# Two expert stages on chunks of 1024 tokens instead of 512, GRU weights loaded before the attention, head sums added block by block

## The chip, the core and the metric

The kernel runs on one core of a Trainium2 chip. The metric is the device time in microseconds. The kernel before took 2214.73 us (median of three runs, 2214.09 to 2214.98). The core has five engines, each with its own instruction queue: TensorE (PE, matmuls into PSUM), VectorE (DVE), ScalarE (ACT), GpSimd (POOL) and SyncE (SP), which here only issues DMAs. They wait for one another through semaphores.

## What is computed

The input is x, 4096 tokens of 128 features, and a 4096 x 4096 adjacency matrix. Four blocks follow one another, each on the layer-normed x, each added to x:

```python
x = x + gnn0(layernorm(x), adj)   # 3 attention heads over adj, two GRU cells
x = x + ffn0(layernorm(x))        # 1 shared and 8 routed experts, width 512, gelu, top 2
x = x + gnn1(layernorm(x), adj)   # adj @ bilinear(h), relu
x = x + ffn1(layernorm(x))        # 8 routed experts, width 256, relu, top 2

# ffn0 (ffn1 has no shared expert, and relu)
h = gelu(einsum('sd,edf->sef', x, W1) + b1)
y = einsum('sef,efd->sed', h, W2) + b2
out = shared + einsum('sed,se->sd', y, mask)   # mask: weights of the two chosen experts

# gnn0
edge_output = gru(adj @ h, h); node_output = gru(sum_of_heads / 3, h)
```

All experts are computed for all tokens; the mask is zero for those not chosen.

## The kernel before

Features lie on the 128 partitions and tokens along the free axis, so x is a tile `xT` of 128 x 4096. The order of the work on every engine is written out by hand, and semaphores tie the engines together; nothing is planned by a scheduler.

**Attention.** `adj` is read in four column blocks of 1024 (`RB`), each in 32 row tiles. For each tile SyncE loads `Ab` (the piece of adj) and `Tt` (weights); GpSimd takes out the diagonal where the tile has one, and in any case raises `a_prep`; ScalarE makes `ss` and rounds `Ab` to bf16 (`Ahi`), after `a_prep`; VectorE makes the remainder `Alo` and the products `ph` and `pl`; TensorE does 24 matmuls. `ph` and `pl` have two buffers each. After a block VectorE and ScalarE evacuate PSUM (`esP`, one part for each head, and `nsT`). After the last block GpSimd adds the three head parts, 512 columns at a time (lines 458 and 460), and SyncE loads the GRU weights and the diagonal `dB`; VectorE and TensorE begin the GRU when `g_in` counts all three.

**GRU.** Sixteen units of 512 columns; TensorE makes four PSUM banks of a unit with fp32 matmuls, ScalarE and VectorE the gates, GpSimd multiplies by `dB` and adds to `xT`.

**Expert stages** (`ffn_tensor`, `ffn_scalar`, `ffn_vector`, `ffn_loads`; k is 0 or 1). First the router: TensorE makes the logits, VectorE picks the two largest, ScalarE makes one `exp` (line 675), TensorE transposes the mask (line 948), ScalarE copies it (`mk8`), and SyncE writes it to DRAM and loads it back broadcast to all partitions (`mB`). Around the router the loop begins early: one expert (k = 0) or two (k = 1) are sent up before the transposes. ScalarE works on four units of them before it comes to `exp`.

The main loop runs over eight chunks of 512 tokens, and in each over nE experts with nF pieces of 128 hidden features (9 and 4, then 8 and 2). For each piece ("unit") TensorE's `up` does three matmuls of 512 columns (bf16 high and low parts) into one PSUM bank out of four; ScalarE's `hidden` applies bias and gelu or relu into `hid` (four buffers) and makes the bf16 copy `hidp` (line 659, every second one in stage 0, where VectorE makes the other, line 1373; all in stage 1); VectorE makes the remainder (line 1382). `down` does three matmuls per unit into the expert's PSUM bank. VectorE's `weighted` adds the bias and multiplies by the mask row (`yT`, line 1401) and adds to `xT` (line 1404). TensorE sends expert e + 1 (stage 0) or e + 2 (stage 1) up before expert e goes down. The mask rows lie in two halves of eight buffers (one chunk each); a chunk's first `weighted` waits for all eight of its half.

The lines below fix how far TensorE may run ahead; `act_done` starts at `HB` = 4.

```python
act.sem_inc(act_done[k], HB)
pe.wait_ge(act_done[k], q * (nE * nF) + j + 1)       # up: a free PSUM slot
act.wait_ge(hid_lo[k], q * (nE * nF) + j + 1)        # hidden: a free hid buffer
pe.wait_ge(hid_lo[k], q * (nE * nF) + HB + (e + 1) * nF)   # down: all units of the expert split
```

Of the kernel before, what the change touches and what calls it, by code (L numbers as in the profile page):

```python
# [9 lines left out]
ALU = mybir.AluOpType  # L10
# [3 lines left out]
ds = bass.ds  # L14
# [9 lines left out]
HB = 4  # L24
TS = 4
# [31 lines left out]
def build(nc, a, out):  # L57
    with ExitStack() as ctx:
# [110 lines left out]
        gruW = sb("gruW", [P, 4, 3 * P], F32, 32)  # L169
        gruB = sb("gruB", [P, 4, 3], F32, 39)  # L170
        gbr = sb("gbr", [P, 2, 2], F32, 39.5)
# [5 lines left out]
        Wr = sb("Wr", [P, NE], F32, 56)  # L177
        rb2 = sb("rb2", [P, 2, NE], F32, 56.25)
# [86 lines left out]
        mB_in = [S("mB_in00", "mB_in01"), S("mB_in10", "mB_in11")]  # L265
# [14 lines left out]
        def _(sp):  # L280
# [85 lines left out]
            sp.dma_start(gruW[:, :, :], a["gruW"]).then_inc(g_in, 16)  # L366
            sp.dma_start(gruB[:, :, :], a["gruB"]).then_inc(g_in, 16)
            sp.dma_start(dB[:, :], diag_d.partition_broadcast(P)).then_inc(g_in, 16)

            def ffn_loads(k, nE, nF):  # L370
# [11 lines left out]
                sp.dma_start(mk_d[k][:, 0:2 * CH], mk8[:, 0:2 * CH]).then_inc(r_out, 16)  # L382
                sp.wait_ge(r_out, 32 * k + 16)
                def weights(s, q):
                    for e in range(NE):
                        sp.dma_start(mB[:, NE * s + e, :], mk_d[k][e, ds(q * CH, CH)].partition_broadcast(P)
                                     ).then_inc(mB_in[k][s], 16)

                weights(0, 0)
                sp.wait_ge(r_mk8, 4 * k + 4)  # L390
                sp.dma_start(mk_d[k][:, 2 * CH:], mk8[:, 2 * CH:]).then_inc(r_out, 16)
                sp.wait_ge(r_out, 32 * k + 32)
                sp.wait_ge(mB_in[k][0], 16 * NE)
                weights(1, 1)
# [7 lines left out]
            sp.wait_ge(dve_ffn0, NC * (2 * NE + 1))  # L402
# [14 lines left out]
            sp.wait_ge(dve_ffn1, NC * 2 * NE)  # L417
# [6 lines left out]
        def _(pool):  # L424
# [12 lines left out]

            for rb in range(NRB):
# [96 lines left out]
        def _(act):  # L535
# [111 lines left out]
            def ffn_scalar(k, nE, nF, func):  # L647
# [4 lines left out]

                act.sem_inc(act_done[k], HB)
                ring = (12, 8)[k]

                def high(q, j):
                    act.wait_ge(act_done[k], q * (nE * nF) + HB + j + 1)
                    act.wait_ge(down_done[k], q * nE + j // nF + 1)
# [27 lines left out]
                for j in range(HB, nE * nF):  # L686
                    hidden(NC - 1, j)
# [865 lines left out]
```

## Time and profile before

The profiled execution took 2213.51 us; its span from the first to the last instruction is 2211.7 us. The stages by their place in it:

| stretch, us | what | TensorE busy | VectorE busy | granted clock |
|---|---|---|---|---|
| 380 to 1080 | attention | 665.5 | 608.8 | 0.98 |
| 1080 to 1094 | last evacuation, loads for the GRU | 0.8 | 4.1 | 0.64 |
| 1094 to 1190 | GRU | 90.3 | 59.9 | 0.96 |
| 1214 to 1246 | router, first expert stage | 24.5 | 16.8 | 0.68 |
| 1246 to 1618 | loop of the first expert stage | 366.6 | 325.5 | 1.00 |
| 1779 to 1955 | adj @ bilinear | 174.4 | 142.1 | 0.99 |
| 1990 to 2030 | router, second expert stage | 25.0 | 18.0 | 0.76 |
| 2030 to 2204 | loop of the second expert stage | 159.0 | 158.3 | 1.00 |

From the page:

```profile
PE 1821.4 (82%) x8950; PEld 875.2 (40%) x9101; DVE 1692.5 (77%) x1792; ACT 1398.9 (63%) x1767; POOL 187.9 (8%) x154
PE   4221573799999999999798899999987789997997
DVE  4555427788898888888467688888859988855898
PEclk7555788899999999999897899999989999988999
```

The first line is busy time and share of the span of each engine with its number of instructions (PEld is TensorE's weight load, which lies beside its matmuls). The others cut the span into 40 equal slices: a digit is the busy share in tenths, in the last line the granted TensorE clock, where 10 tenths are 2.4 GHz and 5 are 1.2 GHz. An engine's idle time costs nothing unless another waits for it.

### The profile page before, as it was taken

How to read it: one execution, taken by the hardware profiler on the slowest of the kernel's cores; microseconds unless marked ns; L12 is line 12 of the kernel's file. 1: busy time of each engine (PE TensorE's matmuls, PEld its weight loads, DVE VectorE, ACT ScalarE, POOL GpSimd, SP SyncE). 2: the span in 40 equal slices, each digit the busy share in tenths (PEclk: the TensorE clock that was granted, in tenths of full speed). 3: DMA queues.
4: the chain of work that ended last, by engine and by line, in shares of the span. 5: the costliest groups of instructions: out<-in, count | busy, mean ns of one | idle time of the engine just before them, and what ended most of it. 6: DMA issues, size and time to landing. Idle time of an engine off the chain costs nothing.

```text
span 2211.7 us, 30420 instructions
## 1 busy us (share of the span) xinstructions
PE 1821.4 (82%) x8950; PEld 875.2 (40%) x9101; DVE 1692.5 (77%) x1792; ACT 1398.9 (63%) x1767; POOL 187.9 (8%) x154
## 2 busy tenths in 40 slices
PE   4221573799999999999798899999987789997997
PEld 4111221344444444444345444444452234463332
DVE  4555427788898888888467688888859988855898
ACT  1777006778787787788334566776645567626885
POOL 0000001100000000000442000000017710000000
PEclk7555788899999999999897899999989999988999
DMA  5997025454545544554600311232030079814532
GB/s 166 429 427 319 0 80 205 162 155 150 170 150 156 169 148 154 170 151 149 238 0 0 79 38 39 48 60 45 1 123 11 0 305 429 366 39 81 98 89 76
DMA packets 79575, 313.89 MB, mean 142 GB/s; under 512 B 13958, under 2 KB 14438, under 8 KB 69494
## 3 DMA queue, kind: packets, MB, share of 16 engines
q1 hardware_dynamic: 79500, 312.98, 42.5%
q8 instruction: 36, 0.59, 0.1%
q14 instruction: 39, 0.32, 0.1%
HBM read 297.88 MB, written 15.08 MB: 142 GB/s over the span
## 4 chain that ended last, share of the span: by engine, by line
PE 40%; DVE 9%; POOL 3%; issue 3%; ACT 1%; DMA 1%; DVEq 0%; SPq 0%; POOLq 0%; ACTq 0%
PE psum L926 9%; PE psum L936 8%; PE psum L1008 7%; PE psum L876 7%; POOL halves L487 3%; DVE hidp L1382 2%; DVE xT L1404 2%; DVE yT L1401 2%; DVE prod L1441 2%; PE psum L900 1%; PE psum L902 1%; PE psum L748 1%; PE psum L914 1%; PE psum L743 1%; PE psum L754 1%
## 5 line engine op out<-in xcount | busy, mean ns | idle before, releaser
L589 ACT ACTIVATE ss<-KR,dpt 128x1024 bf16<-128x1024 int16 x384 | 413.1, 1138 | 112.0 <-DVE pl L1274 111.2
L876 PE MATMUL psum<-ph,Tt 128*128 128x512 bf16 x1502 | 411.9, 380 | 8.8 <-DVE pl L1274 7.0
L665 ACT ACTIVATE hid<-psum,fB 128x512 f32<-128x512 f32 x416 | 271.2, 686 | 151.2 <-PE psum L926 108.0
L936 PE MATMUL psum<-hidp,fW 128*128 128x512 bf16 x1215 | 289.2, 381 | 23.3 <-DVE hidp L1382 17.3
L926 PE MATMUL psum<-hTp,fW 128*128 (+1 forms) x1224 | 295.3, 384 | 5.9 <-ACT mk L679 2.8
L1382 DVE TENSOR_TENSOR hidp<-hid,hidp 128x512 bf16<-128x512 f32 x416 | 268.7, 687 | 26.7 <-DVE xT L1404 10.4
L1271 DVE TENSOR_TENSOR ph<-ss,Ahi 128x3072 bf16<-128x3072 bf16 x128 | 225.2, 1760 | 61.9 <-PE psum L876 60.2
L876 PE MATMUL psum<-pl,Tt 128*128 128x512 bf16 x752 | 225.9, 380 | 0.8
L876 PEld LDWEIGHTS psum<-ph,Tt 128*128 128x128 bf16 x1536 | 150.5, 98 | 190.4 <-issue 6.4
L1274 DVE TENSOR_TENSOR pl<-ss,Alo 128x3072 bf16<-128x3072 bf16 x128 | 224.2, 1751 | 0.0
L936 PEld LDWEIGHTS psum<-hidp,fW 128*128 128x128 bf16 x1248 | 117.6, 98 | 183.2 <-issue 42.1
L926 PEld LDWEIGHTS psum<-hTp,fW 128*128 128x128 bf16 x1248 | 123.2, 99 | 155.1 <-issue 12.1
L1268 DVE TENSOR_TENSOR Alo<-Ab,Ahi 128x1024 bf16<-128x1024 f32 x128 | 163.2, 1275 | 17.3 <-ACT Ahi L599 17.3
L876 PE MATMUL psum<-Ahi,Tt 128*128 128x512 bf16 x503 | 151.0, 380 | 24.2 <-DVE Alo L1268 20.3
L659 ACT ACTIVATE hidp<-hid 128x512 bf16<-128x512 f32 x272 | 163.4, 624 | 0.0
L1468 DVE TENSOR_TENSOR A4lo<-A,A4hi 128x4096 bf16<-128x4096 f32 x32 | 141.3, 4425 | 21.5 <-ACT A4hi L719 21.5
L541 ACT ACTIVATE Ar<-Ar 128x4096 f32<-128x4096 f32 x32 | 115.7, 3617 | 58.2 <-DVE keep L1102 58.2
L719 ACT ACTIVATE A4hi<-A 128x4096 bf16<-128x4096 f32 x32 | 115.4, 3616 | 50.0 <-PE psum L1008 23.2
L599 ACT ACTIVATE Ahi<-Ab 128x1024 bf16<-128x1024 f32 x128 | 133.3, 1042 | 6.4 <-issue 6.3
L785 PE MATMUL psum<-uvs,keep 128*128 128x18 bf16 x1024 | 32.7, 176 | 122.0 <-DVE keep L1102 122.0
L1008 PE MATMUL psum<-A4hi,Xb 128*128 128x512 bf16 x512 | 115.9, 379 | 0.0
L986 PE MATMUL psum<-bw,h3b 128*128 128x512 bf16 x368 | 86.1, 385 | 34.2 <-DVE prod L1441 32.5
(228 smaller groups left out, 2110.6 us busy)
## 6 DMA issues: line engine op xcount, KB each, us to landing
Ar<-in_adjT SPq DMA_DIRECT2D x32, 2048.0 KB, 12.9
Ab<-in_adjT SPq DMA_DIRECT2D x128, 512.0 KB, 4.1
A<-in_adjT SPq DMA_DIRECT2D x32, 2048.0 KB, 11.1
Tt<-T_d SPq DMA_DIRECT2D x128, 256.0 KB, 2.6
mB<-mk_d SPq DMA_DIRECT2D x128, 256.0 KB, 7.6
T_d<-tb SPq DMA_DIRECT2D x32, 256.0 KB, 2.0
RD<-rden_d SPq DMA_DIRECT2D x12, 512.0 KB, 5.3
fWs<-in_W SPq DMA_DIRECT2D x2, 2304.0 KB, 16.5
```

Source lines behind the costliest of these rows:

```text
L589: last = nc.scalar.activation(ss[s % 2][:, h, :], KR[:, h, rb * RB:(rb + 1) * RB], ACT.Sigmoid, scale=STEP, bias=dpt[:, ds(t * HEADS + h, 1)])
L659: nc.scalar.activation(hidp[j % ring][:, 0, :], hid[j % HB][:, :], ACT.Copy).then_inc(hid_hi[k], 1)
L665: nc.scalar.activation(hid[j % HB][:, :], psum[:, j % HB, :], func, bias=fB1[:, j:j + 1]).then_inc(act_done[k], 1)
L876: last = nc.tensor.matmul(psum[:, 2 * h + q, :], Tt[s % AS][:, h, w, :], mv[:, q * CH:(q + 1) * CH], start=fresh and k == 0, stop=False, s ...
L926: last = nc.tensor.matmul(psum[:, j % HB, :], fW[0][x][:, j * P:(j + 1) * P], hTp[y][:, nlast(q)], start=(w == 0), stop=(w == 2))
L936: last = nc.tensor.matmul(psum[:, HB + e % dn, :], fW[1][x][:, j * P:(j + 1) * P], hidp[j % ring][:, y, :], start=(f == 0 and w == 0), sto ...
L1008: last = nc.tensor.matmul(psum[:, q, :], Xb[w][:, ds(n, 1), :].rearrange("p o f -> p (o f)"), mv[s][:, q * CH:(q + 1) * CH], start=False, ...
L1268: V.tensor_tensor(Alo[s % AS][:, :], Ab[s % AS][:, :], Ahi[s % AS][:, :], ALU.subtract).then_inc(a_lo, 1)
L1271: V.tensor_tensor(ph[s % 2][:, :, :], ss[s % 2][:, :, :], Ahi[s % AS][:, :].unsqueeze(1).to_broadcast([P, HEADS, RB]), ALU.mult).then_inc( ...
L1274: V.tensor_tensor(pl[s % 2][:, :, :], ss[s % 2][:, :, :], Alo[s % AS][:, :].unsqueeze(1).to_broadcast([P, HEADS, RB]), ALU.mult).then_inc( ...
L1382: V.tensor_tensor(hidp[j % ring][:, 1, :], hid[j % HB][:, :], hidp[j % ring][:, 0, :], ALU.subtract).then_inc(hid_lo[k], 1)
L1468: V.tensor_tensor(A4lo[s][:, :], A4[s][:, :], A4hi[s][:, :], ALU.subtract).then_inc(l_lo, 1)
```

## The change

1. **Expert stages.** A chunk is 1024 tokens (`CW`), so the loop has four rounds (`NW`). A unit takes two PSUM banks: the `up` slots are banks 0-1 and 2-3, two instead of four, and an expert's output banks 4-5 or 6-7, two instead of three or four. Each weight is used by two matmuls in a row (`for b in range(2)`). ScalarE's, VectorE's instructions and the mask DMAs are 1024 columns wide and half as many. `hid` stays four buffers, each twice as wide, and `hidp` has nine. `down` waits unit by unit.
2. **Mask rows.** Eight buffers `mB`, each refilled for the next chunk when its expert is done; `weighted` waits for pairs of them.
3. **GRU weights** are loaded to another place, ahead of `rden_d` and so of the attention; `dB` is counted by `x_in`, for which only GpSimd waits. TensorE no longer waits for the third head's evacuation.
4. **Head sums**: `head_sums(rb - 1)` behind the tiles of block rb, the last one at the end.

```diff
-            pe.wait_ge(es_out, HEADS * NRB + 1)
+            pe.wait_ge(es_out, HEADS * NRB)
...
-            sp.dma_start(dB[:, :], diag_d.partition_broadcast(P)).then_inc(g_in, 16)
+            sp.dma_start(dB[:, :], diag_d.partition_broadcast(P)).then_inc(x_in, 16)
...
+            def head_sums(rb):
+                pool.wait_ge(es_out, HEADS * rb + HEADS + 1)
+                for q in range(rb * RB // CH, (rb + 1) * RB // CH):
+                    c = slice(q * CH, (q + 1) * CH)
+                    pool.tensor_tensor(esT[:, c], esT[:, c], esP[:, 1, c], ALU.add).then_inc(es_add, 1)
+                    pool.wait_ge(es_add, q + 1)
+                    pool.tensor_tensor(esT[:, c], esT[:, c], esP[:, 2, c], ALU.add).then_inc(es_ok, 1)
...
+                if rb > 0:
+                    head_sums(rb - 1)
+
+            head_sums(NRB - 1)
+            pool.wait_ge(x_in, 48)
...
-                with sp.Fori(1, NC // 2) as i:
-                    for s in range(2):
-
-                        sp.wait_ge(y_used[k], (2 * i + s - 1) * nE + (3, 4)[k])
-                        weights(s, 2 * i + s)
+                with sp.Fori(1, NW) as q:
+                    for e in range(NE):
+                        sp.wait_ge(y_used[k], (q - 1) * nE + (nE - NE) + e + 1 + 2)
+                        weights(q, e)
...
-                act.sem_inc(act_done[k], HB)
-                ring = (12, 8)[k]
+                act.sem_inc(act_done[k], 2)
+                ring, hold = (9, 8)[k], (3, 4)[k]
...
-                    nc.scalar.activation(hid[j % HB][:, :], psum[:, j % HB, :], func,
+                    nc.scalar.activation(hid[j % HB][:, :], flat[:, j % 2 * CW:j % 2 * CW + CW], func,
...
-                            last = nc.tensor.matmul(psum[:, j % HB, :], fW[0][x][:, j * P:(j + 1) * P],
-                                                    hTp[y][:, nlast(q)], start=(w == 0), stop=(w == 2))
+                            for b in range(2):
+                                last = nc.tensor.matmul(psum[:, j % 2 * 2 + b, :], fW[0][x][:, j * P:(j + 1) * P],
+                                                        hTp[y][:, ds(q * CW + b * CH, CH)], start=(w == 0),
+                                                        stop=(w == 2))
...
-                    pe.wait_ge(hid_lo[k], q * (nE * nF) + HB + (e + 1) * nF)
-                    pe.wait_ge(y_used[k], q * nE + e + 1)
+                    pe.wait_ge(y_used[k], q * nE + e + (2 if nE % 2 and e == 0 else 1))
                     for f in range(nF):
                         j = e * nF + f
+                        pe.wait_ge(hid_lo[k], q * (nE * nF) + HB + j + 1)
...
-                    if e == nE - NE:
-                        dve.wait_ge(mB_in[k][half], (i + 1) * (16 * NE))
+                    if p >= 0 and p % 2 == 0:
+                        dve.wait_ge(mB_in[p // 2], (k * NW + q + 1) * 32)
```

How the order moves at three places. On **SyncE**, between the end of the T_d stores and the first load of the attention, before:

```order
L332 COMPARE_AND_BRANCH
L339 ISA
L342 DMA rden_d<-den_94 96x128 [waits t_out0,t_out1,t_out2,t_out3,rden_ok]
L346 UNCONDITIONAL_BRANCH [waits rden_out]
L347 UNCONDITIONAL_BRANCH
```

and now:

```order
L337 COMPARE_AND_BRANCH
L344 ISA
L346 DMA gruW<-in_gruW 128x1536 [waits t_out0,t_out1,t_out2,t_out3]
L347 DMA gruB<-in_gruB 128x12
L349 DMA rden_d<-den_94 96x128 [waits rden_ok]
L353 UNCONDITIONAL_BRANCH [waits rden_out]
L354 UNCONDITIONAL_BRANCH
```

Two loads stand ahead of `rden_d`, whose landing the first `Ab` waits for.

On **GpSimd**, behind the tiles of the second column block (`a_hi` says that ScalarE has rounded a tile), before:

```order
L443 REGISTER_ALU [waits a_hi]
L443 COMPARE_AND_BRANCH
L439 REGISTER_ALU
L439 COMPARE_AND_BRANCH
L439 UNCONDITIONAL_BRANCH
L443 UNCONDITIONAL_BRANCH
```

and now:

```order
L453 REGISTER_ALU [waits a_hi]
L453 COMPARE_AND_BRANCH
L449 REGISTER_ALU
L449 COMPARE_AND_BRANCH
L444 TENSOR_TENSOR esP<-esP 128x512 [waits es_out]
L446 TENSOR_TENSOR esP<-esP 128x512 [waits es_add]
L444 TENSOR_TENSOR esP<-esP 128x512
L446 TENSOR_TENSOR esP<-esP 128x512 [waits es_add]
L449 UNCONDITIONAL_BRANCH
L453 UNCONDITIONAL_BRANCH
```

Four additions stand between the last tile of a block and the first tile of the next.

On **TensorE**, in the loop of the first expert stage, from the last unit of `up` to `down` (`fW_171` to `fW_174`, and `fW_178` to `fW_181` now, are the high and low parts of both weights, `hTp` those of the input, `hidp` those of the hidden units), before:

```order
L926 MATMUL psum<-hTp_162,fW_171 128x512 [waits act_done_0]
L926 MATMUL psum<-hTp_163,fW_171 128x512
L926 MATMUL psum<-hTp_162,fW_172 128x512
L932 ISA [waits hid_lo_0]
L936 MATMUL psum<-hidp_175,fW_173 128x512 [waits y_used_0]
L936 MATMUL psum<-hidp_175,fW_173 128x512
L936 MATMUL psum<-hidp_175,fW_174 128x512
L936 MATMUL psum<-hidp_176,fW_173 128x512 x2
L936 MATMUL psum<-hidp_176,fW_174 128x512
L936 MATMUL psum<-hidp_177,fW_173 128x512 x2
L936 MATMUL psum<-hidp_177,fW_174 128x512
L936 MATMUL psum<-hidp_178,fW_173 128x512 x2
```

and now:

```order
L933 MATMUL psum<-hTp_162,fW_178 128x512 [waits act_done_0]
L933 MATMUL psum<-hTp_162,fW_178 128x512
L933 MATMUL psum<-hTp_163,fW_178 128x512 x2
L933 MATMUL psum<-hTp_162,fW_179 128x512 x2
L939 ISA
L945 MATMUL psum<-hidp_182,fW_180 128x512 [waits hid_lo_0,y_used_0]
L945 MATMUL psum<-hidp_182,fW_180 128x512 x3
L945 MATMUL psum<-hidp_182,fW_181 128x512 x2
L945 MATMUL psum<-hidp_183,fW_180 128x512 [waits hid_lo_0]
L945 MATMUL psum<-hidp_183,fW_180 128x512 x3
L945 MATMUL psum<-hidp_183,fW_181 128x512 x2
L945 MATMUL psum<-hidp_184,fW_180 128x512 [waits hid_lo_0]
```

Each matmul has a second one with the same weight behind it, and `down` waits at each unit.

## Rows read from the trace of the kernel before

**Rows 1.** stages: window, length, busy PE, PEld, DVE, ACT, POOL, PEclk, DMA, GB/s

```profile
1246.00:1618.00 372.00, 366.59 (x1668) 166.45 (x1704) 325.48 (x562) 257.37 (x432) 0.00 (x0) 1.00 0.22 44
2030.00:2204.00 174.00, 159.02 (x688) 64.04 (x700) 158.30 (x240) 136.42 (x231) 0.00 (x0) 1.00 0.39 78
```

**Rows 2.** timeline of the first expert stage: TensorE, then ScalarE

```profile
1264.27 2.75 PE L926 MATMUL psum<-hTp,fW 128*128 x11
1266.86 1.46 PE L936 MATMUL psum<-hidp,fW 128*128 128x512 bf16 x6
...
1265.18 1.33 ACT L665 ACTIVATE hid<-psum,fB 128x512 f32<-128x512 f32 x2 [1.65 <-PE psum L926]
...
1291.06 1.28 ACT L665 ACT_TABLE_LOAD   x1 [1.64 <-PE psum L926]
```

**Rows 3.** VectorE in the second expert stage: first output, one round, last output

```profile
2021.87 0.75 DVE L1401 SCALAR_TENSOR_TENSOR yT<-psum,fB,mB 128x512 f32<-128x512 f32 x1 [9.63 <-DMA mB<-mk_d]
...
2032.38 1.29 DVE L1382 TENSOR_TENSOR hidp<-hid,hidp 128x512 bf16<-128x512 f32 x2 [0.22 <-DVE xT L1404]
2033.59 0.74 DVE L1401 SCALAR_TENSOR_TENSOR yT<-psum,fB,mB 128x512 f32<-128x512 f32 x1
2034.37 0.69 DVE L1404 TENSOR_TENSOR xT<-xT,yT 128x512 f32 x1
...
2202.83 0.75 DVE L1401 SCALAR_TENSOR_TENSOR yT<-psum,fB,mB 128x512 f32<-128x512 f32 x1
```

**Rows 4.** timeline where the attention ends and the GRU begins

```profile
1082.80 1.22 DVE L1285 TENSOR_TENSOR esP<-esP,RD 128x1024 f32<-128x1024 f32 x1
1093.38 1.00 DVE L1299 TENSOR_TENSOR gbr<-gruB 128x2 f32<-128x2 f32 x1 [9.37 <-DMA dB<-diag_d]
1093.69 2.07 PE L900 MATMUL psum<-nsT,gruW 128*128 x2 [13.21 <-DVEq L1301]
```

**Rows 5.** SyncE before the attention; columns start us, us, engine, line, operation

```profile
388.92 0.35 SPq L342 DMA_DIRECT2D rden_d<-den  x1
391.22 0.37 SPq L352 DMA_DIRECT2D Ab<-in_adjT  x1
```

**Rows 6.** DMA issues by size; last number us from issue to landing

```profile
gruW<-in_gruW SPq DMA_DIRECT2D x1, 768.0 KB, 4.1
```

**Rows 7.** the tile esP: its instructions, ns min/median/max

```profile
L458 POOL TENSOR_TENSOR esP<-esP x8: 1259/1260/1271, 1084.1 to 1102.0; 128x512 f32<-128x512 f32 x8
L1282 DVE TENSOR_TENSOR esP<-psum,RD x8: 1214/1220/1225, 570.0 to 1081.7; 128x1024 f32<-128x1024 f32 x8
L604 ACT ACTIVATE esP<-psum x4: 1018/1018/1019, 571.0 to 1081.4; 128x1024 f32<-128x1024 f32 x4
```

**Rows 8.** VectorE's timeline where the second column block ends

```profile
728.13 1.22 DVE L1268 TENSOR_TENSOR Alo<-Ab,Ahi 128x1024 bf16<-128x1024 f32 x1
740.25 2.35 DVE L1282 TENSOR_TENSOR esP<-psum,RD 128x1024 f32<-128x1024 f32 x2 [1.75 <-PE psum L876]
746.28 1.22 DVE L1268 TENSOR_TENSOR Alo<-Ab,Ahi 128x1024 bf16<-128x1024 f32 x1 [2.53 <-ACT Ahi L599]
```

**Rows 9.** timeline, GpSimd and VectorE on a tile with a diagonal block

```profile
401.95 0.92 POOL L449 TENSOR_TENSOR Ab<-Ab,cst 128x128 f32 x1 [2.68 <-ACT Ahi L599]
402.48 1.47 DVE L1268 TENSOR_TENSOR Alo<-Ab,Ahi 128x1024 bf16<-128x1024 f32 x1
```

**Rows 10.** stages view again (columns as Rows 1), just after the attention

```profile
1084.00:1086.00 2.00, 0.00 (x0) 0.00 (x0) 0.01 (x1) 0.00 (x0) 1.83 (x2) 0.50 0.53 65
```

**Rows 11.** begin of the second expert stage: TensorE, then SyncE

```profile
1990.17 4.90 PE L926 MATMUL psum<-hTp,fW 128*128 128x512 bf16 x11 [0.94 <-issue]
2000.68 5.49 PE L948 MATMUL psum<-cst,s 128*8 128x128 f32 x27 [5.62 <-DVE s L1366]
...
2005.44 7.39 SPq L386 DMA_DIRECT2D mB<-mk_d  x8
```

**Rows 12.** TensorE's stall in the first expert stage

```profile
1345.89 2.33 PE L936 MATMUL psum<-hidp,fW 128*128 128x512 bf16 x10 [1.17 <-DVE hidp L1382]
```

More of the change, by code:

```diff
@@ L24 @@
 HB = 4
+CW = 1024
+NW = N // CW
 TS = 4
@@ L167, in build @@
         dB = sb("dB", [P, N], F32, 104)
-        gruW = sb("gruW", [P, 4, 3 * P], F32, 32)
-        gruB = sb("gruB", [P, 4, 3], F32, 39)
-        gbr = sb("gbr", [P, 2, 2], F32, 39.5)
+        gruW = sb("gruW", [P, 4, 3 * P], F32, 56)
+        gruB = sb("gruB", [P, 4, 3], F32, 62)
+        gbr = sb("gbr", [P, 2, 2], F32, 62.125)
         gR = [sb(f"gR{i}", [P, CH], F32, 40 + 2 * i) for i in range(2)]
@@ L274, in nlast, with wide @@
             return ds(q * CH, CH)
+        def wide(q):
+            return ds(q * CW, CW)
         block = ctx.enter_context(nc.Block())
@@ L340, in _ @@
                 sp.sem_inc(seen, 1)
+            sp.dma_start(gruW[:, :, :], a["gruW"]).then_inc(g_in, 16)
+            sp.dma_start(gruB[:, :, :], a["gruB"]).then_inc(g_in, 16)
             sp.wait_ge(rden_ok, 1)
@@ L680, in ffn_scalar @@
                                          ACT.Copy).then_inc(r_mk8, 1)
-                with act.Fori(0, NC - 1) as q:
+                with act.Fori(0, NW - 1) as q:
                     for j in range(HB, nE * nF):
@@ L686, in ffn_scalar @@
                 for j in range(HB, nE * nF):
-                    hidden(NC - 1, j)
+                    hidden(NW - 1, j)
             ffn_weights(0, *FFN0)
@@ L908, in ffn_tensor @@
             def ffn_tensor(k, nE, nF):
-                ring, dn, lag = (12, 8)[k], (3, 4)[k], (1, 2)[k]
+                ring, hold, lag = (9, 8)[k], (3, 4)[k], (1, 2)[k]
                 pe.wait_ge(r_in, 96 * (k + 1))
@@ L916, in ffn_tensor @@
                 last.then_inc(r_ps, 1)
-                pe.sem_inc(down_done[k], ring // nF)
+                pe.sem_inc(down_done[k], hold)
                 pe.wait_ge(f_lo, (NC + 2) * (k + 1))
@@ L952, in ffn_tensor @@
                 pe.wait_ge(r_mk8, 4 * k + 4)
-                with pe.Fori(0, NC - 1) as q:
+                with pe.Fori(0, NW - 1) as q:
                     for e in range(nE):
@@ L1411, in chunk @@
                             high(q + (e + lag) // nE, (e + lag) % nE)
-                        weighted(q, i, half, e, f)
+                        weighted(q, e, f)
                     assert f.n == per
@@ L1416, in ffn_vector @@
                     high(0, e)
-                with dve.Fori(0, NC // 2 - 1) as i:
-                    for half in range(2):
-                        chunk(2 * i + half, i, half, True)
-                chunk(NC - 2, NC // 2 - 1, 0, True)
-                chunk(NC - 1, NC // 2 - 1, 1, False)
+                with dve.Fori(0, NW - 1) as q:
+                    chunk(q, True)
+                chunk(NW - 1, False)
             lt_vector(0, lambda: low_weights(0, *FFN0))
```

91 lines of the change are left out of this document (40 added, 51 removed).

## The prediction

> **What bounds the kernel now.** I read the views in this order: the page (busy shares, then the 40 slices), the table of stages, the timelines where the stages touch, and the prices of single instructions. The page says TensorE is busiest, but that is an average. The table of stages separates the places the change touches. In the first expert stage TensorE is busy 366.6 of 372 us at the full granted clock (1.00), VectorE 325 [rows 1]: TensorE is the bound, and shorter work elsewhere gives at most the 5.4 us of its idle time. In the timeline [rows 2] the reader is to see twelve matmuls per 2.59 us (1264.27 to 1266.86), 0.216 us each, and ScalarE idle for 1.65 us before each unit. In the second stage TensorE (159.0) and VectorE (158.3 of 174 us) look alike [rows 1]; the order in time decides it: VectorE repeats split pair, yT, xT with gaps of 0.22 us, 63 rounds from 2021.87 to 2202.83, 2.87 us each, against 12 x 0.216 = 2.59 us of matmuls [rows 3]. There VectorE is the bound. Its first output also waits 9.63 us for the mask rows mB [rows 3]. Between attention and GRU, VectorE's work ends at 1084.02, but gbr waits 9.37 us for the DMA of dB and TensorE starts at 1093.69 [rows 4].
>
> **Start of the attention.** SyncE now issues gruW and gruB ahead of rden_d, and the first Ab follows only when rden_d has landed: today issued 388.92, Ab at 391.22 [rows 5]. At least the two issues are added, about 0.35 us each by the like row [rows 5]: +0.7. At most rden_d lands behind all of gruW's 768 KB, which took 4.1 us [rows 6]: gruW issued at 388.9 lands at 393.0, the small ones 0.4 to 0.9 behind, Ab at 394.0, +2.8. I take **+2.8**, since the 4.1 us belong to this very transfer; range 0.7 to 4. The Trainium skill, "DMA: Bandwidth & Descriptors", section Queues, rings and completion order, says that each DMA engine consumes one queue's descriptors in ring order, which would make it 2.8 and not 0.7; no row here separates the two.
>
> **Head sums.** The two additions per 512 columns (1.26 us each on GpSimd [rows 7]) move out of the gap behind the attention into its inside: four behind the tiles of each later block. Behind them in GpSimd's queue stands a_prep of the next block's first tile; ScalarE's Ahi waits for it, VectorE's Alo for that, TensorE for both. What hides them: at a block's end VectorE stands 1.75 us before it evacuates, and 2.53 us before the next Alo [rows 8]. Unhindered the four take 5.0 us, about a tile, and cost nothing. But GpSimd and VectorE hinder each other: a GpSimd multiplication ran 0.92 us while VectorE worked, and the VectorE subtraction after it 1.47 us [rows 9] against 1.22 [rows 8]. If every one of the four takes turns with a VectorE instruction, they take 10 us, VectorE loses some 4 us, its evacuation slips by 3 us from 740.25 to 743.3 and ends at 746.8; the next Alo starts there instead of at 746.28 [rows 8]: 0.55 us. Two boundaries have sums: **+1.1**; range 0 to 7.
>
> **GRU.** The weights are there, and dB is waited for by GpSimd only, whose first product with it comes after the first GRU unit has gone through TensorE, ScalarE and VectorE; dB's DMA is issued no later than today, so that wait stays hidden. TensorE waits for the second evacuation (over at 1082.9, as 1.22 us before 1084.0 begins the third [rows 4]) and for gbr's release behind it, 1084.0 to 1085.1. I take 1084.0 instead of 1093.69: -9.7. The granted clock is 0.50 (1.2 GHz) from 1084 on [rows 10], and the first two matmuls took 2.07 us at it [rows 4]; if the work begins before it has fallen, up to 2 us go as well: -1. Together **-10.7**; range -8.5 to -12.5. The last block's sums (5 us of GpSimd) lie beside the first GRU units.
>
> **First expert stage.** Prices at 1024 elements: VectorE's split 1.22 [rows 8] against 0.69 [rows 3] (half a pair of 1.29, and a little overlap; xT's row is 0.69 too), so +0.53 for 512 elements more, where two instructions would have paid 0.69 again. With a PSUM operand 1024 elements take 1.22 as well [rows 7]. ScalarE's hidden unit: between 1.02, the copy of that shape [rows 7], and 1.33, two of today's [rows 2]; I take 1.10.
> Begin, worked out on the second stage's times, which the rows show: ScalarE's queue has the first four units ahead of the router's exp. They are 24 matmuls now, not 12 (4.90 us at the low clock [rows 11], so 2.57 per new unit), and there are two PSUM slots instead of four. Unit 1 ends 1992.7, unit 2 1995.3; ScalarE ends their activations at 1996.7, the two copies (about 1.0 each, by the 1.02 [rows 7]) at 1998.7, and units 3 and 4, which TensorE has ready by then, with their copies at 2002.9. Today the matmuls end at 1995.07 and one activation (0.69) and two copies (about 0.6 each) behind them at 1997. So exp comes 6.0 later, and the transposes, which today wait 5.62 us for that chain until 2000.68 [rows 11], too. In the first stage ScalarE makes only every second copy, so one fewer behind the last unit: +5.3, between 4 (the clock rises midway) and 7.
> Loop: 12 matmuls went ahead of it: -2.6. New: the third unit of an expert needs the slot of the first. That unit ends 1.30 us after the beginning, ScalarE starts 0.26 later (1264.92 to 1265.18 [rows 2]), takes 1.10, and the release needs 0.05 to 0.3, say 0.13: 2.78 against 2.59, a wait of 0.19 us. 36 experts: +6.8 (range 2 to 15). The activation table is loaded again at each loop top, 1.28 us [rows 2], today in the shade of four slots; now in front of that wait: three times 1.28, +3.8. VectorE's stall at its loop top, which TensorE feels as 1.17 us [rows 12], comes at two such places; the split parts now lie ready some 8 us before TensorE wants them, so it goes: -2. VectorE's busy share of 325 in 372 us [rows 1] only falls: no bound.
> Tail: two instructions, each 0.53 longer: +1.1. Sum 5.3 - 2.6 + 6.8 + 3.8 - 2.0 + 1.1 = **+12.4**; range +4 to +18.
>
> **Second expert stage.** Begin 6.0 later, so mB's first issue moves from 2005.44 [rows 11] to 2011.4. But the first output waits for two buffers of 512 KB now, not for eight of 256 KB, which took from 2005.4 to 2021.8, 16 us [rows 3, 11]: 1 MB has landed about 2020. By then VectorE has split the third expert's units (matmuls from about 2014, their two activations and copies behind, 7.4 us to the last split) and reaches the output at 2021.8, as today. A round is then, for VectorE, 2.87 + 4 x 0.53 = 4.99 us (against 5.74 for two of today's); for TensorE 24 x 0.216 = 5.18. TensorE becomes the bound. Within an expert there are only two units, so the slot of the first is long free. 29 rounds of 5.18 (150.2) and three outputs of 2.7 without new units (8.1): 2180.1, with 1.5 for small stalls 2181.6; today 2202.83 + 1.47 = 2204.3. **-22.7**; range -12 to -26. The refills are hidden: 4 MB in 41 us against the 2 MB in 16 us that went through.
>
> **Sum.** 2.8 + 1.1 - 10.7 + 12.4 - 22.7 = -17.1. The profiled execution took 2213.5 us (span 2211.7), 1.2 below the median of 2214.7; so 2196.4 on its scale and 2197.6 as a median.
>
> **Rivals.** *VectorE stays the bound of the second stage*, at 5.5 us a round, because handoffs of longer pieces leave gaps: 29 x 0.32 = +9.3, 2207. For it: 4.99 is only 4% under 5.18; against: today's gaps are 0.22 [rows 3].
> *The two slots are enough in the first stage*: no 6.8, so 2191. For it: 0.19 is a difference of small numbers.
> *Slower: long instructions save nothing.* If ScalarE needs 1.33 for a two-bank unit, its answer comes after 3.0 us, and the third and fourth unit lose 0.52 together, 18.7 for 6.8, with begin and tail +13.3; if VectorE too pays double, its round is 5.74 and the second stage loses 29 x 0.56 = 16.2: 2197.6 + 13.3 + 16.2 = 2227. It decides slower from about half of these surcharges on. Against it: 1.22 and 1.02 at 1024 elements, from PSUM too [rows 7].
> *GpSimd loses the shared turns at the block ends*: its sums come only where VectorE stands, a_prep 10 us late, the evacuation with it, about 8 us for each of two boundaries: +14.9, 2212.5. The row for it is the 0.92 us [rows 9]; against it, it got its turn right after the running instruction. The Trainium skill, "SBUF — State Buffer", section Who interferes with whom, states such a lock for VectorE instructions with two SBUF inputs against GpSimd reads, for the whole instruction, the later one waiting; by that rule turns alternate and the term stays at 1.1.
> *The GRU starts no earlier*, some other wait being last: +10.7, 2208. Against it, the row names dB and nothing else ended after 1084.
>
> **How the numbers follow.** Forecast 0.60; VectorE's bound 0.12; slots enough 0.12; slower 0.06; GpSimd 0.04; GRU 0.06. This kernel's measurement tells 0.2%, 4.4 us, from no change. Faster (under 2210.3): 0.60 less 0.02, 0.11, 0.12, 0.01, 0.06: 0.88. Within: 0.04. Slower: 0.06 and 0.02 that no case names: 0.08. The forecast's own terms spread it over 2190 to 2206; for 8 in 10 I reach to 2187 and 2209.
>
> **What would show it.** The GRU's first matmul at about 1087 (1084 and 2.8); Ab's first issue near 394; TensorE waiting for hid at the third unit of each expert, with 1.3 us more at three table loads; expert transposes 5 to 6 us after today's distance; a second stage with TensorE at 5.18 us a round and VectorE's output every 5.18. Wrong it is if ScalarE's units take over 1.2 us, if VectorE's rounds exceed 5.2, or if GpSimd's sums stretch far over 10 us.

## The result, and the profile after

The changed kernel took 2188.94 us (median; before 2214.47 in the same comparison), a ratio of 0.9884, 95% interval 0.9864 to 0.9903: 25.5 us faster where 17.1 were forecast. The medians count one execution of 5035 us here (without it 2188.68), one of 4025 us in the second experiment (without it 2210.54) and one of 3404 us in the seventh (without it 2209.38); ratios and intervals leave them out. The profiled executions took 2213.51 and 2189.21 us (spans 2211.7 and 2187.4).

The stages view of the changed kernel (columns as in [rows 1]), for the two expert stages:

```profile
1246.00:1616.00 370.00, 367.38 (x1679) 158.61 (x1677) 291.72 (x275) 212.97 (x209) 0.00 (x0) 1.00 0.11 39
2023.00:2175.00 152.00, 150.42 (x697) 67.99 (x695) 140.36 (x118) 118.40 (x116) 0.00 (x0) 1.00 0.28 94
```

In the second stage TensorE is now busy 150.4 of 152 us and VectorE 140.4, where before they had stood level [rows 1]: the bound has moved to TensorE. The timelines show it. First come VectorE's rows: the splits ahead of the first output, the first two outputs, two outputs near the end, and the last row. Then come TensorE's rounds without a wait (12 matmuls per row) and its one stall at the end:

```profile
2020.21 2.36 DVE L1391 TENSOR_TENSOR hidp<-hid,hidp 128x1024 bf16<-128x1024 f32 x2 [7.51 <-ACT hidp L665]
2022.48 1.28 DVE L1410 SCALAR_TENSOR_TENSOR yT<-psum,fB,mB 128x1024 f32<-128x1024 f32 x1
2023.91 1.23 DVE L1412 TENSOR_TENSOR xT<-xT,yT 128x1024 f32 x1
2025.72 2.36 DVE L1391 TENSOR_TENSOR hidp<-hid,hidp 128x1024 bf16<-128x1024 f32 x2 [0.58 <-ACT hidp L665]
2028.00 1.27 DVE L1410 SCALAR_TENSOR_TENSOR yT<-psum,fB,mB 128x1024 f32<-128x1024 f32 x1
...
2162.35 1.28 DVE L1410 SCALAR_TENSOR_TENSOR yT<-psum,fB,mB 128x1024 f32<-128x1024 f32 x1
...
2167.53 1.27 DVE L1410 SCALAR_TENSOR_TENSOR yT<-psum,fB,mB 128x1024 f32<-128x1024 f32 x1
...
2179.48 1.23 DVE L1412 TENSOR_TENSOR xT<-xT,yT 128x1024 f32<-128x1024 f32 x1
...
2041.17 2.75 PE L933 MATMUL psum<-hTp,fW 128*128 x12
2043.76 2.75 PE L945 MATMUL psum<-hidp,fW 128*128 128x512 bf16 x12
2046.35 2.75 PE L933 MATMUL psum<-hTp,fW 128*128 x12
...
2175.36 2.76 PE L945 MATMUL psum<-hidp,fW 128*128 128x512 bf16 x12 [1.94 <-DVEq L1413]
```

2046.35 less 2041.17 is 5.18 us a round of TensorE, and VectorE's outputs come at the same distance (2162.35, 2167.53). The first output no longer waits for mB [rows 3]; what VectorE waits for ahead of it, 7.51 us, is ScalarE's copy.

In the first stage, TensorE's 24 matmuls of an expert's units start 5.32 us ahead of its outputs', not 5.18: 0.14 us are lost on the slot. ScalarE's row shows why: it leaves the first unit at 1264.23, and the third unit, which needs that slot, could have begun at 1264.16, twelve matmuls of 0.216 behind 1261.57. The page gives 3.8 us of TensorE's waits to `hid`: three table loads, each felt as 1.25 us; the row at 1243.28 is one of them.

```profile
1261.57 5.49 PE L933 MATMUL psum<-hTp,fW 128*128 x24
1266.89 5.34 PE L945 MATMUL psum<-hidp,fW 128*128 128x512 bf16 x24
1272.07 5.49 PE L933 MATMUL psum<-hTp,fW 128*128 x24
...
1263.12 1.11 ACT L671 ACTIVATE hid<-psum,fB 128x1024 f32<-128x1024 f32 x1 [4.20 <-PE psum L933]
...
1243.28 2.76 PE L933 MATMUL psum<-hTp,fW 128*128 x12 [1.25 <-ACT hid L671]
```

```profile
L933 PE MATMUL psum<-hTp,fW 128*128 (+1 forms) x1248 | 291.4, 384 | 7.8 <-ACT hid L671 3.8
```

Where the attention ends (answering to [rows 4]) and where it begins (to [rows 5]):

```profile
1086.39 2.35 DVE L1292 TENSOR_TENSOR esP<-psum,RD 128x1024 f32<-128x1024 f32 x2 [4.36 <-PE psum L882]
1089.19 1.37 PE L906 MATMUL psum<-nsT,gruW 128*128 x2 [2.84 <-DVE esP L1292]
...
391.27 0.35 SPq L346 DMA_DIRECT2D gruW<-in_gruW  x1
391.67 0.42 SPq L347 DMA_DIRECT2D gruB<-in_gruB  x1
392.14 0.43 SPq L349 DMA_DIRECT2D rden_d<-den  x1
396.74 0.36 SPq L359 DMA_DIRECT2D Ab<-in_adjT  x1
```

From rden_d's issue to the first Ab it is 4.60 us, before 2.30 [rows 5]; with the two issues ahead of it (0.87) that is +3.2. The DMA view has rden_d landing 3.8 us behind its issue (1.5 before), 0.6 us after gruW.

At the blocks' ends GpSimd's sums and VectorE's work stretch each other (GpSimd, then VectorE, then TensorE's wait there, in this trace and in the one before the change):

```profile
733.57 1.62 POOL L444 TENSOR_TENSOR esP<-esP 128x512 f32<-128x512 f32 x1 [87.25 <-ACT Ahi L605]
735.27 2.13 POOL L446 TENSOR_TENSOR esP<-esP 128x512 f32<-128x512 f32 x1
737.36 2.79 POOL L444 TENSOR_TENSOR esP<-esP 128x512 f32<-128x512 f32 x1
740.23 2.66 POOL L446 TENSOR_TENSOR esP<-esP 128x512 f32<-128x512 f32 x1
...
733.99 2.29 DVE L1278 TENSOR_TENSOR Alo<-Ab,Ahi 128x1024 bf16<-128x1024 f32 x1
736.20 2.82 DVE L1281 TENSOR_TENSOR ph<-ss,Ahi 128x3072 bf16<-128x3072 bf16 x1
738.95 2.82 DVE L1284 TENSOR_TENSOR pl<-ss,Alo 128x3072 bf16<-128x3072 bf16 x1
741.78 2.19 DVE L1278 TENSOR_TENSOR Alo<-Ab,Ahi 128x1024 bf16<-128x1024 f32 x1
...
747.23 2.34 DVE L1292 TENSOR_TENSOR esP<-psum,RD 128x1024 f32<-128x1024 f32 x2
...
752.13 1.23 DVE L1278 TENSOR_TENSOR Alo<-Ab,Ahi 128x1024 bf16<-128x1024 f32 x1 [1.43 <-ACT Ahi L605]
...
747.28 0.59 PE L882 MATMUL psum<-Ahi,Tt 128*128 128x512 bf16 x2 [1.21 <-ACT nsT L609]
```

```profile
741.42 0.59 PE L876 MATMUL psum<-Ahi,Tt 128*128 128x512 bf16 x2 [1.21 <-ACT nsT L603]
```

Four sums take 9.3 us, a split 2.29 where it took 1.22. The four sums alone would be 5.0 us and VectorE's four instructions beside them 5.6 (as they are from 746.28 to 751.89 before), together 10.6; both are done within 10.3 us (733.57 to 743.89), about as if they took turns. VectorE loses 4.3 us. It pays with idle time: the 1.75 us before its evacuation are gone [rows 8], about 1.2 us of waits before its products too, the evacuation comes 1.1 us later (13.24 us behind the split at 733.99; before, 12.12 behind the one at 728.13), and of the 2.53 us behind it 1.43 are left. The next block's first split comes where it came before (18.1 us behind the same split in both). TensorE loses nothing: 13.29 us from that split to its wait for nsT, which is 1.21 us, in both traces.

The whole difference of the two spans, by stretches. The first keep mask is VectorE's first comparison of a piece of adj with zero, the node-sum evacuation ScalarE's copy of nsT out of PSUM, and the router's result the first instruction of VectorE on the logits:

| stretch | before | after | change |
|---|---|---|---|
| start to the first keep mask | 57.51 | 59.97 | +2.5 |
| first keep mask to the last node-sum evacuation | 1023.02 | 1026.42 | +3.4 |
| from there to the GRU's first matmul | 13.16 | 2.80 | -10.4 |
| GRU's matmuls | 84.61 | 84.36 | -0.3 |
| end of the GRU to the router's result (layer-norm) | 46.76 | 43.56 | -3.2 |
| router's result to the first stage's last matmul | 391.95 | 399.52 | +7.6 |
| from there to the second router's result | 372.25 | 374.98 | +2.7 |
| second router's result to the last xT | 215.04 | 189.10 | -25.9 |
| output | 7.40 | 6.69 | -0.7 |

The sum is -24.3, the difference of the spans.

Single rows of this table are less sure than the sum. Five other traces run code that is the same up to the GRU as in the kernel before, but for the head sums in one of them (experiments 1, 3, 7, 10, 11). In them the stretch from the evacuation to the GRU took 13.6 to 15.0 us, not 13.16, with dB landing 8.9 to 10.3 us behind its issue and not 8.5. From the first Ab to the last evacuation the fourteen traces took either 686.5 to 686.7 or 689.3 to 689.6 us, whatever the kernel.

### The profile page after: what moved, and what is told of

Read it like the earlier page. It is cut to its first block, busy times and chain, and to the rows that moved or that the text cites. A ratio compares the mean times of both kernels' runs of the same rounds, so it can differ in the third digit from the quotient of the medians.

```text
span 2187.4 us, 28393 instructions
## 1 busy us (share of the span) xinstructions
PE 1826.6 (84%) x9101; PEld 870.7 (40%) x9101; DVE 1658.1 (76%) x1380; ACT 1341.0 (61%) x1419; POOL 201.2 (9%) x154
## 4 chain that ended last, share of the span: by engine, by line
PE 48%; DVE 4%; POOL 3%; ACT 1%; issue 1%; POOLq 0%; ACTq 0%; DVEq 0%
PE psum L933 13%; PE psum L945 12%; PE psum L1018 8%; PE psum L882 7%; POOL halves L493 3%; DVE prod L1447 2%; PE psum L906 1%; PE psum L908 1%; PE psum L754 1%; PE psum L920 1%; PE psum L749 1%; PE psum L760 1%; PE psum L911 1%; PE psum L910 1%; PE psum L958 0%
## 5 line engine op out<-in xcount | busy, mean ns | idle before, releaser
L882 PE MATMUL psum<-ph,Tt 128*128 128x512 bf16 x1536 | 417.1, 380 | 6.6 <-DVE pl L1284 6.6
L671 ACT ACTIVATE hid<-psum,fB 128x1024 f32<-128x1024 f32 x208 | 227.1, 1112 | 186.1 <-PE psum L933 186.0
L945 PE MATMUL psum<-hidp,fW 128*128 128x512 bf16 x1248 | 280.2, 379 | 1.9 <-DVEq L1413 1.9
L1391 DVE TENSOR_TENSOR hidp<-hid,hidp 128x1024 bf16<-128x1024 f32 x208 | 245.4, 1221 | 26.2 <-ACT hidp L665 24.6
L933 PEld LDWEIGHTS psum<-hTp,fW 128*128 128x128 bf16 x1248 | 117.5, 99 | 170.2 <-ACT hid L671 32.0
L1278 DVE TENSOR_TENSOR Alo<-Ab,Ahi 128x1024 bf16<-128x1024 f32 x128 | 168.3, 1315 | 18.6 <-ACT Ahi L605 18.6
L945 PEld LDWEIGHTS psum<-hidp,fW 128*128 128x128 bf16 x1248 | 122.0, 98 | 149.5 <-DVEq L1413 2.4
L665 ACT ACTIVATE hidp<-hid 128x1024 bf16<-128x1024 f32 x136 | 139.6, 1051 | 0.0
```

What stands on the lines that cost most here:

```text
L665: nc.scalar.activation(hidp[j % ring][:, 0, :], hid[j % HB][:, :], ACT.Copy).then_inc(hid_hi[k], 1)
L671: nc.scalar.activation(hid[j % HB][:, :], flat[:, j % 2 * CW:j % 2 * CW + CW], func, bias=fB1[:, j:j + 1]).then_inc(act_done[k], 1)
L882: last = nc.tensor.matmul(psum[:, 2 * h + q, :], Tt[s % AS][:, h, w, :], mv[:, q * CH:(q + 1) * CH], start=fresh and k == 0, stop=False, s ...
L933: last = nc.tensor.matmul(psum[:, j % 2 * 2 + b, :], fW[0][x][:, j * P:(j + 1) * P], hTp[y][:, ds(q * CW + b * CH, CH)], start=(w == 0), s ...
L945: last = nc.tensor.matmul(psum[:, 4 + e % 2 * 2 + b, :], fW[1][x][:, j * P:(j + 1) * P], hidp[j % ring][:, y, b * CH:b * CH + CH], start=( ...
L1278: V.tensor_tensor(Alo[s % AS][:, :], Ab[s % AS][:, :], Ahi[s % AS][:, :], ALU.subtract).then_inc(a_lo, 1)
```

## The experiments

Medians; the kernel before stood at 2214.95 in the first four, 2215.22 in the next four, 2214.73 in the ninth and 2215.36 in the twelfth, and the intervals reach 2 to 4 us to either side, so the small terms are read from the traces. The theory after the comparison: the terms are the forecast's, with other sizes, and the layer-norm's 3.2 us are a sixth.

**1. Only the wide expert stages** (the first two parts of the change on the kernel before).

```diff
+ CW = 1024; hid, yT, mB[8], hidp[9] of CW columns; Fori over NW in ffn_*
  gruW, gruB, dB: loaded behind the attention; head sums: in one row, as before
```

> Both expert stages on chunks of 1024 with the eight refilled buffers; GRU weights and head sums as before. Theory (time is lost in the first expert stage and won in the second): router result to layer-norm +8.7 us in the first stage, -25.9 in the second, so -17 us in all, and if the 2.4 us by which the changed kernel's first input landed late belong to every rewritten program, -15. The prediction's own terms (+12.4, -22.7) give -10.3. Rival (the second stage gained only because the GRU part changed what came before it): less than 15 us won from router to output in the second stage here.

Measured 2199.89 (ratio 0.9927, 0.9914 to 0.9941): -15.1, the theory's number for a late start. That it fits so well is in part luck: its own trace began 4.3 us late and got 2.2 of them back by the last evacuation. The two stages gave +9.7 and -26.0: from the second router's result to the last xT it took 189.08 us. The gain of that stage stands alone; the rival falls.

**2. Only the GRU part.**

```diff
+ gruW, gruB issued ahead of rden_d, dB on x_in
- pe.wait_ge(es_out, HEADS * NRB + 1)
+ pe.wait_ge(es_out, HEADS * NRB)
```

> GRU weights loaded as the attention begins, the diagonal behind the attention, TensorE waits for one evacuation fewer; experts and head sums as before. Theory: +3.2 at the attention's start, -10.4 at the GRU's first matmul, and the granted clock of 1.00 in the layer-norm behind it is a consequence of the early start, -3.3: -10.5 us in all. Rival (that clock moved by chance or by another part): -7.2 us, with the clock of 1.00 in the layer-norm's last 10 us only where it was before. With a late start of 2.4 us as in the changed kernel, 2.4 less.

Measured 2210.73 (0.9983, 0.9974 to 0.9992): -4.2, less than either expected. The GRU does start 2.80 us behind the last node sums, but its matmuls take 88.45 us. GpSimd's timeline, then VectorE's wait, then the only wait among TensorE's GRU matmuls:

```profile
1088.22 1.26 POOL L458 TENSOR_TENSOR esP<-esP 128x512 f32<-128x512 f32 x1 [20.48 <-DVE esP L1284]
...
1107.52 1.26 POOL L460 TENSOR_TENSOR esP<-esP 128x512 f32<-128x512 f32 x1
1111.06 1.26 POOL L469 TENSOR_TENSOR gU<-gU,dB 128x512 f32<-128x512 f32 x1 [2.28 <-DVE gU L1319]
...
1107.71 1.62 DVE L1317 TENSOR_TENSOR gU<-hT,gM 128x512 f32<-128x512 f32 x1 [5.19 <-POOLq L463]
...
1113.79 1.12 PE L899 MATMUL psum<-nsT,gruW 128*128 x2 [3.78 <-DVE gM L1310]
```

All sixteen sums stand in one row ahead of the line (463) with which GpSimd frees the buffers gU; VectorE's first use of them waits 5.19 us for it, and TensorE 3.78 us for VectorE. Its layer-norm's stretch took 47.15 us: the clock of the theory was not there either.

**3. Only the head sums by block.**

```diff
+ if rb > 0: head_sums(rb - 1)      # in the attention, as changed
+ head_sums(NRB - 1)
```

> Head sums on GpSimd at every row block, all else as before. Theory (TensorE has slack at the block boundaries, so the stretched turns of GpSimd and VectorE cost it nothing): +0.3 us, and TensorE's waits at the boundaries as before. The prediction had +1.1 (three boundaries of 0.36). Rival (the sums themselves had held up the GRU): -1 us or more. If any rewritten program starts its first input 2.4 us late, that comes on top.

Measured 2214.84 (1.0000, 0.9992 to 1.0009): nothing. The stretched turns are free: from the first keep mask to the last evacuation it is 1023.11 us, before 1023.02. (The prediction's +1.1 were two boundaries of 0.55, not three of 0.36 as the expectation has it.) That the whole is zero hides two differences of the single traces: the wait for dB and the GRU took 2.7 us longer here, the layer-norm 3.2 us less, and the seventh experiment's trace, which has no such sums, has the same two.

**4. The first stage narrow again.**

```diff
+ ffn_loads_n, ffn_scalar_n, ffn_tensor_n, ffn_vector_n: the functions of before, for k = 0
  ffn_* of the change for k = 1; all else as changed
```

> The changed kernel with the first expert stage put back to chunks of 512 and its two sets of mask buffers; the second stage wide, GRU weights and head sums as changed. Theory (the wide form costs where TensorE already set the pace, and pays where VectorE did): 8.7 us less than the changed kernel, 2180 us. Rival (the eight refilled buffers or the wide tiles are worth the same in both stages, and the first stage's loss came from the loop tops' clock): within 2 us of the changed kernel, 2189.

Measured 2178.82 (0.9834, 0.9821 to 0.9846): 10.1 us under the changed kernel; the rival falls. From the first router's result (1216.89) to the second (1981.23) it is 764.3 us; changed 774.5, before 764.2. The wide first stage costs 10.2 us.

```profile
1216.89 0.42 DVE L1487 TENSOR_TENSOR lg<-psum,rb 128x256 f32<-128x256 f32 x1 [2.81 <-PE psum L998]
1981.23 0.42 DVE L1578 TENSOR_TENSOR lg<-psum,rb 128x256 f32<-128x256 f32 x1 [2.70 <-PE psum L1052]
```

**5. GRU weights at the attention's end** (on the fourth).

```diff
- gruW, gruB issued ahead of rden_d
+ gruW, gruB issued behind the last tile of the attention, ahead of xT
```

> The fourth experiment's kernel (second expert stage wide, GRU and head sums as changed) with the two GRU weight transfers moved from the attention's begin to its end, right ahead of the input's own reload. Theory (their only cost was that the small transfer of the denominators queued behind them): the first load of the attention goes out 2.3 us behind the denominators' issue again instead of 4.6, the GRU still starts 2.8 us after the last node sum, and the whole is 3.2 us shorter than that kernel, 2175.6. Rival (the weights come too late or hold up the reload of the input): the GRU starts 1 us or more later, and nothing is won.

Measured 2175.47 (0.9822, 0.9809 to 0.9836), 3.35 less than the fourth. SyncE again:

```profile
389.54 0.35 SPq L352 DMA_DIRECT2D rden_d<-den  x1
391.83 0.37 SPq L362 DMA_DIRECT2D Ab<-in_adjT  x1
```

2.29 us, and the GRU starts 2.80 behind the last node sums as before. The attention's term was this queue alone, and was not needed. In all six traces with the weights ahead of rden_d the first Ab was issued 5.4 to 5.6 us behind the first of these issues, in all eight others 2.3.

**6. The exponential behind the second unit** (on the changed kernel).

```diff
- hidden(0, 0..3); Exp
+ hidden(0, 0); hidden(0, 1) without its copy; Exp; its copy; hidden(0, 2..3)
```

> The changed kernel with the router's exponential on ScalarE behind the second wide unit instead of the fourth, in both expert stages. Theory (the begin of each stage waits for ScalarE: 6.3 and 8.2 us of VectorE's idle time in the rows before the selection's second half): the mask transposes come 3.0 us earlier in the first stage, of which a second reload of Gelu's table takes 1.3 on ScalarE's path, and 5 us in the second; 5 to 8 us in all, 2182. Rival (the copies of the selection on ScalarE, which wait behind the other two units, take its place): under 2 us.

Measured 2181.13 (0.9851, 0.9836 to 0.9866): -7.8. From router to transposes 10.81 us in both stages, not 14.71 and 16.60. The first stage gains 5.2 to its last matmul, since the transposes come 3.9 us earlier and Gelu's table is loaded once, ahead of the loop, and never in it; the second only 2.4 by its end, for the reason that experiment 8 shows. ScalarE, behind the exponential:

```profile
1227.43 1.28 ACT L671 ACT_TABLE_LOAD   x1
```

**7. The first masks apart** (on the kernel before, second stage).

```diff
- dve.wait_ge(mB_in[k][half], (i + 1) * (16 * NE))            # at e == 0
+ even chunks: at e == 0 two masks, at e == 2 the other six
```

> The kernel before, where in the second expert stage the first two experts of each even chunk wait for their own two masks alone, not for all eight; nothing else. Theory (VectorE sets the pace of that stage, 2.85 us an expert of 512, and the 9.63 us wait for masks is only its begin): it does two experts inside that wait, -5.7 us, and the rounds keep their length, so most of the changed kernel's -25.9 there comes from the wide instructions. Rival (the mask transfers themselves were what the stage lacked): more than 12 us.

Measured 2209.66 (0.9971, 0.9960 to 0.9983): -5.6. VectorE's timeline at the first outputs:

```profile
2015.87 0.74 DVE L1409 SCALAR_TENSOR_TENSOR yT<-psum,fB,mB 128x512 f32<-128x512 f32 x1
...
2018.88 0.74 DVE L1409 SCALAR_TENSOR_TENSOR yT<-psum,fB,mB 128x512 f32<-128x512 f32 x1
...
2025.30 0.75 DVE L1409 SCALAR_TENSOR_TENSOR yT<-psum,fB,mB 128x512 f32<-128x512 f32 x1 [3.43 <-DMA mB<-mk_d]
```

Two experts fit into the wait, no more; the rival falls. The third still waits 3.43 us for masks, so this kernel shows what a part of the wait is worth, not the whole of 9.63. Of the second stage's 25.9 us, then, 16 to 20 (25.9 less 9.6, or less 5.7) belong to the long instructions by this estimate, and the rest to the mask buffers. No kernel with long instructions and the old mask halves was run.

**8. All that paid together** (fourth, fifth, and the sixth in the wide stage).

```diff
  the fifth experiment's kernel
+ the sixth experiment's order in ffn_scalar, k = 1
```

> The fourth experiment's kernel with both of the last two edits: GRU weights at the attention's end, and in the wide second stage the exponential behind the second unit. Theory (the terms add, since they lie in different stages): 3.2 and 4 to 5.8 us less than that kernel, 2170 to 2172. Rival (the masks' transfers, which now lie on the path to the first output, keep the second stage's begin where it is): 2175.

Measured 2172.85 (0.9812, 0.9798 to 0.9825), the fastest here, but only 2.6 under the fifth. That lies just above the theory's 2170 to 2172 and under the rival's 2175, and what is missing has another reason than the rival's: no output waits for masks. TensorE's timeline:

```profile
1988.53 1.91 PE L1097 MATMUL psum<-cst,s 128*8 128x128 f32 x16 [2.18 <-DVE s L1606]
1992.99 2.60 PE L1097 MATMUL psum<-cst,s 128*8 128x128 f32 x16 [2.56 <-ACT mk L770]
1996.98 4.70 PE L1072 MATMUL psum<-hTp,fW 128*128 x12 [1.39 <-ACT mk L770]
```

The selection's copies now stand on ScalarE behind units 3 and 4 (2.56 us), and the twelve matmuls behind them took 4.70 us instead of the changed kernel's 2.76: the granted clock was 0.50 from 1996 to 2000 us here, 1.00 from 2015 to 2018 in the changed kernel. The sixth experiment's trace has the same in this stage, 2.56 and 4.75 us.

**9. GRU part and head sums together**, experts as before.

```diff
  the second experiment's kernel
+ the third experiment's head sums
```

> The kernel before with the GRU part and the head sums by block together, both expert stages as before. Theory (the sixteen sums in one row on GpSimd end 20.6 us after the last evacuation and hold up the first product of an early GRU by 3.8 us, so the block sums are worth nothing alone and about 4 us here): -4.2 - 0.1 - 3.8 = -8 us at least; if the parts make up the changed kernel's whole gain together with the wide stages' -15.1, -10.9. Rival (the 6 us by which the three single edits fell short of the changed kernel lie between the wide stages and the rest): -4.3 us, the sum of the two.

Measured 2204.36 (0.9951, 0.9938 to 0.9965): -10.4; alone they gave -4.2 and -0.1. With the first experiment's -15.1 that is the changed kernel's -25.5. The rival falls: the missing 6 us lie between these two parts. The GRU's matmuls take 84.36 us again, 4.1 less than in the second experiment. The layer-norm's stretch is the other difference of the two traces, 43.57 here and 47.15 there; it comes from the granted clock, and the next three experiments ask whose that is.

**10, 11. The kernel before, twice more.**

> The kernel before once more, for one more trace. Theory (the higher granted clock in the layer-norm behind the GRU comes and goes from execution to execution and belongs to no edit): the stretch from the GRU's last matmul to the router's result takes 43.6 us here, as in five of the changed traces and in the kernel whose only edit lies behind it. Rival (it belongs to an edit): 46.8 us, as in the first trace of this kernel.

> The same kernel a third time, with the same two expectations for the layer-norm behind the GRU (43.6 or 46.8 us), and for the first input: 57.5 us to the first keep mask if that start is the kernel's own, anything from 57.5 to 61.8 if it is the execution's.

2215.10 and 2214.42. The first keep mask came at 60.80 and 58.94 us: the late start is the execution's own. The layer-norm's stretch took 46.74 both times, against the theory. But the seventh kernel, the same up to there, took 43.60, so the rival, which gave the shorter stretch to an edit, falls too.

**12. The changed kernel shifted by 5 us.**

```diff
+ if rb == NRB - 1: four tensor_tensor(dB[...], RD[:, 0], RD[:, 1], mult)   # in evacuate
```

> The changed kernel with four idle products on VectorE (1.22 us each, their result unused) ahead of the last evacuation, so that the GRU and all behind it start 5 us later. What the traces so far show: where the GRU's last matmul ended at 1168.4 to 1174.3 or at 1183.4 to 1184.6 us, the stretch from there to the router's result took 43.6 us; where it ended at 1175.9 to 1180.5, 46.7 to 47.2, whatever had been edited. Theory (the granted clock there goes by where in time the work falls, so the changed kernel's 3.2 us in the layer-norm come with its earlier GRU): the GRU ends near 1178, the stretch takes 46.7, and the whole is 5 + 3.2 us longer than the changed kernel, 2197. Rival (it goes by something that the edits changed): 43.6 again, 2194.

Measured 2198.34 (0.9913, 0.9897 to 0.9928; single runs 2192.1 to 2199.1). The GRU started 7.85 us behind the last node sums (+5.05), but this execution began late (first keep mask at 64.41), so the GRU ended at 1182.2, beside the place meant; the stretch took 43.6. The test missed and settles nothing; its runs scatter over 7 us, and only one has a trace.

## Why the prediction was right, and where its sizes were off

The forecast's case came true: all five mechanisms are there, and no rival is. The time was at the range's lower end, and below the 2190 to 2206 over which the forecast's terms alone spread it, because four terms missed in one direction (1.1, 2.1, 3.2 and 3.2 us). The last of them is in no term, and what sets it stayed open; without it the time would have been near 2192.

- **Start of the attention, +2.8:** +3.2 by the issues, 3.35 by the fifth experiment. The Trainium skill, "DMA: Bandwidth & Descriptors", section Queues, rings and completion order, has the DMA engines take one queue's descriptors in order. The trace agrees: rden_d landed 0.6 us behind gruW, and the term was nearer to 2.8 than to 0.7.
- **Head sums, +1.1:** 0. The sums took 9.3 us and VectorE lost 4.3, as assumed (10 and 4), but its evacuation slipped by 1.1 us and not by 3, since the idle time before its products covered a part that the term had left out. What the term did not see either is their use: without them the early GRU is held up by 4 us.
- **GRU, -10.7:** -10.6 (-10.36 at its start, where 9.7 were assumed; of the 1 us for the clock 0.25). The wait that came next was the second evacuation, as named.
- **First stage, +12.4:** +10.3. Begin 3.8 for 5.3; slot 0.145 x 36 = 5.2 for 6.8, since the slot came free 0.06 us behind ScalarE's activation where 0.13 was assumed; table loads 3.75 for 3.8; VectorE's loop tops -2.4 for -2; tail and what follows it +2.7 for +1.1. ScalarE's unit took 1.11 us where 1.10 was assumed. The slot's share is read from the trace alone; no kernel with more slots was run.
- **Second stage, -22.7:** -25.9. The first output came 1.7 us nearer to the router's result, as the masks no longer delayed it and ScalarE's begin cost 5.2 us where 6.0 were assumed, and the rounds ran at 5.18 with none of the 1.5 us for stalls: 158.2 us from the first output to the end for 159.8.
- **Not in the sum:** the layer-norm behind the GRU, -3.2, by a granted clock that reached 1.00 for longer. The forecast held this stretch for unchanged and gave it no term. The last ten us or so of transposes and router ran at 0.84 in the changed kernel and at 0.67 in the kernel before (the second row is from its second trace, experiment 10):

```profile
1203.00:1213.00 10.00, 10.00 (x78) 10.00 (x78) 8.69 (x15) 4.91 (x8) 0.00 (x0) 0.84 0.01 2
```

```profile
1210.00:1220.00 10.00, 10.00 (x64) 10.00 (x63) 8.28 (x14) 4.97 (x8) 0.00 (x0) 0.67 0.01 2
```

What sets it stays open. In all fourteen traces the stretch took 43.6 us where the GRU's last matmul ended before 1174.4 or after 1182.1 us, and 46.7 to 47.2 where it ended between 1175.9 and 1180.5, kernels with and without the edits on both sides. Where it ended after 1182.1 us, the GRU's own matmuls took 85.5 to 85.6 us, not 84.1 to 84.6 (88.45 in the second experiment), so a part of the gain is paid there. A kernel that should end it between the two was tried and missed.

The terms as measured add up to -26.2 us; the late start (+2.5) and the output (-0.7) make the trace's -24.3, but for rounding.

## What to carry to other kernels

Long instructions pay where the engine that issues them sets the pace, and cost where another does: split such a change by stage, read the bound of each, and keep the old form where it was TensorE. Look at what a moved transfer stands ahead of, since a small one behind it waits for its landing, 2.3 us here; and try edits in pairs, because head sums by block were worth nothing alone and about 4 us once the GRU came early.

## What the runs showed of the hardware

- A GpSimd addition of 1.26 us took 1.62 to 2.79 beside VectorE, whose split went from 1.22 to 2.29 and whose products went from 1.75 to 2.82. Both are slowed, neither is shut out, and together they needed 10.3 us for what takes 10.6 one after the other.
- Broadcasts of 4 KB rows (512 KB) landed after 3.7 us in the median; those of 2 KB rows (256 KB) after 7.6. Here twice as many of the short ones wait at once; the two causes were not separated.
- ScalarE's table loads take 1.28 us. Where the exponential is the last table function ahead of the Gelu loop, one stands at the first Gelu of each pass of the loop (1240.8, 1336.9 and 1432.9 us in the changed kernel); where Gelu units stand between the exponential and the loop, as in the sixth experiment, one at 1227.4 us and none in the loop. Where Relu follows the exponential there is none.
- One kernel's first 60 us vary by 3.3 us between executions (57.5 to 60.8 before; up to 64.4 in others), so two single traces should be compared stretch by stretch, and a stretch with its like in a third trace: dB landed 8.5 to 10.3 us behind its issue with no edit to it.
